# The norms' matrices turned by VectorE's blocks and small transfers instead of TensorE's transposes, in a kernel of six transformer layers and a routed gate

## What is computed

```
xn = layernorm(x)                                   # no weights
s  = xn
for i in range(6):
    n = layernorm(s) * ln1_w[i] + ln1_b[i]
    q, k, v = n @ wq[i], n @ wk[i], n @ wv[i]        # 8 heads of 16
    q = softmax(q, over the 16 of a head);  k = softmax(k, over the tokens)
    s = (q @ (k^T v) per head) @ wo[i] + bo[i] + s
    n = layernorm(s) * ln2_w[i] + ln2_b[i]
    h = n @ w1[i];  h = where(h >= 0, h, 0.01 h)     # 512 wide
    s = h @ w2[i] + s
e = argmax(xn @ router_w + router_b);  w = its softmax weight     # 8 experts
out = x + s * silu((xn @ expert_w[e] + expert_b[e]) * w)
```

## Time and profile before

| what | value |
|---|---|
| median of 3 runs | 653.16 us (651.39 to 653.6) |
| the profiled execution | 654.56 us |
| its span, first to last instruction | 652.7 us |
| mean granted TensorE clock | 0.995 of full |
| busy share of the span: TensorE, VectorE, ScalarE, GpSimd | 97%, 81%, 61%, 46% |
| transfers, mean | 44 GB/s |

### The profile page before, as it was taken

The page is one execution under the profiler, slowest core; times in us unless marked ns, Lnnn a source line. Parts: engine busy times, 40 slices in busy tenths (PEclk is TensorE's granted clock), DMA queues, the critical chain, the costliest instruction groups (busy, mean ns, idle before and its releaser), DMA issues.

```text
span 652.7 us, 13026 instructions
## 1 busy us (share of the span) xinstructions
PE 629.9 (97%) x4598; PEld 568.5 (87%) x4598; DVE 530.0 (81%) x1495; ACT 400.8 (61%) x693; POOL 297.9 (46%) x279
## 2 busy tenths in 40 slices
PE   8788989999999999999999999999999999999996
PEld 8677879889889899898898899899899988889885
DVE  6767989878978879879878878788888788988576
ACT  2746647557657566576566576576675665675563
POOL 4442367678433233333223423322432475786643
PEclk9979999999999999999999999999999999999999
DMA  8920000000102002022002021001020010000003
GB/s 288 313 110 2 1 22 30 25 24 30 54 1 66 1 2 66 2 66 65 1 0 57 7 64 48 17 2 39 27 66 17 1 30 20 18 26 21 21 2 130
DMA packets 29175, 29.03 MB, mean 44 GB/s; under 512 B 3265, under 2 KB 24769, under 8 KB 29122
## 3 DMA queue, kind: packets, MB, share of 16 engines
q1 hardware_dynamic: 26640, 24.12, 11.7%
q0 software_dynamic: 2048, 4.20, 2.2%
q10 hardware_dynamic: 434, 0.02, 0.1%
HBM read 17.85 MB, written 10.49 MB: 43 GB/s over the span
## 4 chain that ended last, share of the span: by engine, by line
PE 86%; DVE 6%; ACT 3%; POOL 2%; issue 1%; DMA 1%; DVEq 0%; ACTq 0%
PE psY L440 25%; PE psT L347 12%; PE psH L352 7%; PE psH L353 6%; PE psH L354 6%; PE psM L537 6%; PE psM L486 6%; PE psT L481 6%; PE psS L512 5%; DVE st L717 1%; PE psS L411 1%; DVE hid L976 1%; PE psS L520 1%; DVE qsum L1079 1%; PE psS L525 1%
## 5 line engine op out<-in xcount | busy, mean ns | idle before, releaser
L440 PEld LDWEIGHTS psY<-w_all,hid 128*128 128x128 f32 x1536 | 195.5, 191 | 18.6 <-issue 8.0
L440 PE MATMUL psY<-w_all,hid 128*128 128x128 f32 (+1 forms) x1536 | 203.4, 276 | 0.2 <-DVE X L948 0.2
L1166 POOL TENSOR_TENSOR rstd<-veps,minus_half 128x8 f32<-128x8 f32 x52 | 85.9, 1652 | 181.0 <-DVE veps L734 180.9
L976 DVE TENSOR_TENSOR hid<-psH,hsl 128x512 f32<-128x512 f32 x192 | 131.1, 684 | 33.7 <-ACT hsl L629 30.9
L629 ACT ACTIVATE hsl<-psH 128x512 f32<-128x512 f32 x192 | 114.3, 596 | 53.0 <-PE psH L354 50.4
L647 ACT ACTIVATE xh<-X,shift,rstd 128x128 f32<-128x128 f32 x280 | 116.9, 487 | 0.4 <-POOL shift L1169 0.3
L1220 POOL TENSOR_TENSOR xn_lo<-xn,xn_hi 128x512 fp32r<-128x512 f32 x46 | 57.8, 1278 | 101.3 <-DVE xn_hi L985 101.3
L352 PE MATMUL psH<-xn_hi,w_hi 128*128 128x512 f32 x184 | 86.1, 468 | 4.1 <-POOL xn_lo L1220 1.6
L717 DVE BATCH_NORM_STATS2 st<-X 128x6 f32<-128x128 f32 x384 | 80.6, 278 | 0.1
L353 PE MATMUL psH<-xn_hi,w_lo 128*128 128x512 f32 x184 | 72.9, 396 | 0.0
L354 PE MATMUL psH<-xn_lo,w_hi 128*128 128x512 f32 x184 | 72.5, 394 | 0.0
(11 more groups left out here) (153 smaller groups left out, 1048.3 us busy)
## 6 DMA issues: line engine op xcount, KB each, us to landing
wb<-expert_rows SPq DMA_DIRECT2D x40, 128.0 KB, 2.1
w_all<-in_w_dram SPq DMA_DIRECT2D x12, 256.0 KB, 4.8
sorted_x<-zeros SPq DMA_DIRECT2D x5, 512.0 KB, 6.4
xs<-sorted_x SPq DMA_DIRECT2D x10, 256.0 KB, 2.9
sorted_y<-ys SPq DMA_DIRECT2D x10, 256.0 KB, 2.4
xraw<-in_x_dram SPq DMA_DIRECT2D x4, 512.0 KB, 5.9
out_dram<-xraw SPq DMA_DIRECT2D x3, 512.0 KB, 2.6
expert_rows<-expert_all SPq DMA_DIRECT2D x1, 1024.0 KB, 8.1
```

The costliest lines, as they stand in the source:

```text
L440: last = nc.tensor.matmul(tile(psY, t), tile(hid[:, i % NC, :], t), of_layer(w2_all, l, c * D, D), start=(c == 0 and t == 0), stop=(c == N ...
L976: nc.vector.tensor_tensor(hid[:, i % NC, :], psH[:, i % 2, :], hsl[:, i % 2, :], ALU.max) \
L1166: nc.gpsimd.tensor_tensor(rstd[:, norm, :], veps[:, norm, :], minus_half[:, :], ALU.pow) \
```

## The change

Both norms' matrices are turned without TensorE. VectorE transposes the 32x32 blocks of the normalised matrix into `blocks1` or `blocks2` (one instruction over 128x1024), and sixteen transfers from SBUF to SBUF (`quadrants`), each of 32 partitions by 1 KB (32 KB), put the block rows where they belong, in `turned1` or `turned2`. ScalarE reads these, in another order of columns, for `xnT` and `xn2`. All the transfers are issued by SP, norm 2's of item s-2 ahead of norm 1's of item s, in `slot(s)`. The first item's norm 1 and the last item's norm 2 are still turned by TensorE.

Slots are written out without a hardware loop, and an item now passes through five: norm 1 in slot s (item s), attention (s-1), norm 2 (s-2), the first part of the FFN (s-3), its last four `output` steps (s-4). There are 27 slots, and the steps' order on each engine is new. ScalarE normalises all eight tiles of norm 1 and makes `xn2_hi`. The attention's product goes to `psT` in place of `psM`. The biases of all layers are computed in slot 1; weights and norm parameters are read where they are loaded, without copies. `zeros` shares its memory with `blocks1`, `expert_all` with `blocks2` and `turned2`, `bvm` with `wb`.

The diff, cut to its core:

```diff
+        Q = 32
+        NQ = P // Q
+        blocks1 = sb("blocks1", [P, T])
+        turned1 = sb("turned1", [P, T])
+        turn2 = sb("turn2", [P, 2, T])
+        blocks2, turned2 = turn2[:, 0, :], turn2[:, 1, :]
...
+        def by_block(a):
+            return a.rearrange("p (t i d) -> p i t d", i=NQ, d=Q)
+
+        def by_tile(a):
+            return a.rearrange("p (j t x) -> p t j x", j=NQ, x=Q)
+
+        def natural(a):
+            return a.rearrange("p (t j x) -> p t j x", j=NQ, x=Q)
+
+        def slots(slot):
+            for s in range(1, ITEMS + 4):
+                slot(s)
 
...
+
+            def quadrants(dst, src, name):
+
+                for j in range(NQ):
+                    for i in range(NQ):
+                        sp.dma_start(dst[i * Q:(i + 1) * Q, j * NT * Q:(j + 1) * NT * Q],
+                                     src[j * Q:(j + 1) * Q, i * NT * Q:(i + 1) * NT * Q]).then_inc(sig(name), 16)
+
+            def feature_major1(n):
+
+                if there(n) and n > 0:
+                    sp.wait_ge(sig("blocks1_ready"), n)
+                    wait(sp, "turned1_ready", 16 * NQ * NQ * (n - 1))
+                    wait(sp, "xnT_ready", n)
+                    quadrants(turned1, blocks1, "turned1_ready")
+
+            def feature_major2(n):
+
+                if there(n) and n < ITEMS - 1:
+                    sp.wait_ge(sig("blocks2_ready"), n + 1)
+                    wait(sp, "turned2_ready", 16 * NQ * NQ * n)
+                    wait(sp, "xn2_ready", n)
+                    quadrants(turned2, blocks2, "turned2_ready")
+
+            def slot(s):
+                groups(s)
+                feature_major2(s - 2)
+                feature_major1(s)
+
...
+                attention(s - 2)
+                if s == 2:
+                    normalised_tiles(2)
+                if s == 3:
+                    ranks()
+                output(s - 4, 4)
+                if group_of(s) is not None:
+                    turn_rows(group_of(s))
+                output(s - 4, 5, 6, 7)
+                hidden(s - 3, 0, 1)
+                if group_of(s) is not None:
+                    apply_expert(group_of(s))
+                keys(s - 1)
+                queries(s - 1)
+                if s == 1:
+                    value_bias()
+                if s == 2:
+                    logits(2)
+                hidden(s - 3, 2, 3)
+                keys_by_token(s - 1)
+                if s == 1:
+                    output_bias(0, range(0, 4))
+                    normalised_tiles(0)
+                if s == 2:
+                    normalised_tiles(3)
+                output(s - 3, 0, 1)
+                last_norm2_by_feature(s - 2)
+                key_sums(s - 1)
+                if s == 1:
+                    output_bias(1, range(4, L))
+                    logits(0)
+                    normalised_tiles(1)
+                if s == 2:
+                    logits(3)
+                output(s - 3, 2)
+                hidden(s - 3, 4)
+                context(s - 1)
+                hidden(s - 3, 5)
+                output(s - 3, 3)
+                mixing(s - 1)
+                queries_by_feature(s - 1)
+                if s == 1:
+                    logits(1)
+                hidden(s - 3, 6, 7)
...
+            def attention_input(n):
+
+                if there(n):
+                    wait(act, "k_done", n)
+                    wait(act, "q_done", n)
+                    if n == 0:
+                        act.wait_ge(sig("t1_done"), 1)
+                        act.wait_ge(sig("param_loaded"), 16 * 2)
+                        nc.scalar.activation(xnT[:, :], psT[:, :], ACT.Identity, bias=param(1, n), scale=param(0, n)) \
+                            .then_inc(sig("xnT_ready"), 1)
+                    else:
+                        act.wait_ge(sig("turned1_ready"), 16 * NQ * NQ * n)
+                        nc.scalar.activation(natural(xnT[:, :]), by_tile(turned1[:, :]), ACT.Identity,
+                                             bias=param(1, n), scale=param(0, n)).then_inc(sig("xnT_ready"), 1)
+
+            def hidden_input(n):
+
+                if not there(n):
+                    return
+                wait(act, "xn2_lo_ready", 2 * n)
+                if n == ITEMS - 1:
+                    act.wait_ge(sig("t2_done"), 1)
+                    nc.scalar.activation(xn2[:, :], psM[:, :], ACT.Identity, bias=param(3, n), scale=param(2, n)) \
                         .then_inc(sig("xn2_ready"), 1)
-
...
+                slope(s - 4, 6, 7)
+                hidden_input(s - 3)
+                if group_of(s) is not None:
+                    rows_by_feature(group_of(s))
+                if s == ITEMS + 2:
+                    silu(3)
+                attention_input(s - 1)
+                if s == 1:
+                    normalise_input(2)
+                if s == 2:
+                    feature_major(2)
+                slope(s - 3, 0, 1)
+                norm2(s - 2, 0)
+                norm2(s - 2, 1)
+                norm2(s - 2, 2)
+                exp_keys(s - 1)
+                slope(s - 3, 2)
+                norm2(s - 2, 3)
+                slope(s - 3, 3)
+                if s == ITEMS + 1:
+                    silu(0)
+                    silu(1)
+                keys_by_token(s - 1)
+                if s == 1:
+                    feature_major(0)
+                if s == 2:
+                    feature_major(3)
+                exp_queries(s - 1)
+                norm1(s, 0)
+                norm1(s, 1)
+                norm1(s, 2)
+                norm1(s, 3)
+                if s == 1:
+                    feature_major(1)
+                    normalise_input(3)
+                slope(s - 3, 4, 5)
...
+            def blocks_of_norm1(n):
+
+                if there(n) and n > 0:
+                    dve.wait_ge(sig("xh1_ready"), 4 * (n + 1))
+                    wait(dve, "turned1_ready", 16 * NQ * NQ * (n - 1))
+                    if n == 1:
+                        dve.wait_ge(sig("rows_zeroed"), 16 * (SLOTS // NT))
+                    nc.vector.transpose(blocks1[:, :], by_block(xh1[:, n % 2, :])).then_inc(sig("blocks1_ready"), 1)
+
+            def blocks_of_norm2(n):
+
+                if there(n) and n < ITEMS - 1:
+                    dve.wait_ge(sig("xh2_ready"), 4 * (n + 1))
+                    wait(dve, "turned2_ready", 16 * NQ * NQ * n)
+                    if n == 0:
+                        dve.wait_ge(sig("sorted_rows_out"), 16)
+                    nc.vector.transpose(blocks2, by_block(xh2[:, :])).then_inc(sig("blocks2_ready"), 1)
+
...
+            def slot(s):
+                add_y(s - 4, 0)
+                leaky(s - 4, 6, 7)
+                if s % NBATCH == 3 and s < ITEMS:
+                    stage_w1(s // NBATCH)
+                add_attention(s - 2)
+                if s == 3:
+                    take_ranks()
+                statistics2(s - 2)
+                if s == 3:
+                    count_tokens()
+                add_y(s - 4, 1)
+                if s == ITEMS + 2:
+                    gated(1)
+                statistics1(s, 0)
+                statistics1(s, 1)
+                leaky(s - 3, 0, 1)
+                if s == 3:
+                    pad_counts()
+                if group_of(s) is not None:
+                    expert_bias(group_of(s))
+                key_maxima(s - 1)
+                variances1(s)
+                query_maxima(s - 1)
+                if s == 1:
+                    value_bias()
+                if s == 3:
+                    first_rows()
+                blocks_of_norm2(s - 2)
+                leaky(s - 3, 2, 3)
+                if s == 1:
+                    output_bias(0, 0, 4)
+                if s == 3:
+                    rows_of_tokens()
+                if s == ITEMS + 1:
+                    gated(0)
+                query_sums(s - 1)
+                scale_key_sums(s - 1)
+                if s == 1:
+                    output_bias(1, 4, L)
+                sum_reciprocals(s - 1)
+                mask_context(s - 1)
+                blocks_of_norm1(s)
+                leaky(s - 3, 4, 5)
+                if s == 4:
+                    experts_of_tiles()
+                    top_weights()
+                if s == ITEMS + 2:
+                    gated(2)
+                finish_mix(s - 1)
+                if s == 2:
+                    route()
+                if s == ITEMS + 3:
```

More of the change, by code:

```diff
@@ L220, in xb, with param @@
         def xb(a, b, lo=0, n=T):
[L222 to L268, removed]
+            return a[:, b, lo:lo + n]
+        def param(k, n):
+            return lnp[:, k, n // NBATCH:n // NBATCH + 1]
+        def by_block(a):
[7 more added lines that the diff above has]
+                slot(s)
         block = ctx.enter_context(nc.Block())
@@ new lines, in value_bias, with output_bias @@
+            def value_bias():
+                pe.wait_ge(sig("attn_loaded"), 16 * 4 * (L - 1))
```

(54 more changed lines are left out.)

693 lines of the change are left out of this document (233 added, 460 removed).

## The result

The changed kernel takes 864.57 us (median of 4, 861.92 to 868.23) against 653.38 us for the kernel before (median of 4, 651.39 to 655.71): a ratio of 1.323, interval 1.316 to 1.331. The forecast was 683 us with a range up to 716. The direction was right; the size was far off, 211 us of loss where 30 were forecast.

What follows compares the result with a forecast made beforehand. TensorE's ordered instructions bound the kernel before; after the change, the circle through SP's queue would. Span 21.75 + 81 + 129 + 239.4 + 154.8 + 56.6 = 682.6, + 1.86 - 1.4 = 683 us; range 640 to 716.

Steps and rivals of the forecast that it cites:

- the circle over `keys`: Path from one `keys` start to the next through DVE, SP's 32 issues, landing and `xnT`: 25.8 us a slot.
- the issue interval: SP's queue issues one transfer every 0.472 us, bounds 0.43 to 0.50; last of 32 starts 14.6 us after the first.
- the clock: Rival, 12%: TensorE's clock falls during waits, keys and queries take 7.0 us: 29.3 a slot, 760 in all, 722 if half.
- the first slots: First three steps of the kernel: 27.5 + 26 + 27.5 = 81 us, against 73.6 before.
- the tail: Time after the last key product to the end of the span: kept at 56.6 us.
- The forecast's own sign of being wrong: In SP's queue, an issue interval other than 0.47 us in the changed profile would show the forecast wrong.
- the landing: Last transfer of norm 1, from issue to arrival: 2.1 us, bounds 1.6 to 2.6.
- The nine slots with groups: Slots 9 to 17, where `groups(s)` frees SP at 8.65 and not 7.85 us after `keys`: 26.6 us each.
- the removed transposes: 46 sets of norm transposes leave TensorE, 0.87 us each: 40 us, 1.74 per slot.
- the rival that it costs double: Rival, 8%: the block transpose on DVE costs double, one in the circle adding 1.2 x 22 = 26 us: 709.
- The transfers are quick enough: Rival, 26%: 32 issues and last landing take 15.6 us or less, so no slower; 643 at 14.9 us.
- The transfers don't matter: Rival, 4%: TensorE stays the bound, all 40 us come back, 23.2 a slot, about 615; needs an interval below 0.37.

Runs made afterwards that it cites:

- Kernel 2: The changed kernel with 40 identity transposes in front of each key product, where TensorE otherwise waits: 830.63 us, ratio 1.268.
- kernel 5: The changed kernel with both norms turned by TensorE again, keeping the new orders and five slots, without block transposes or their transfers: 673.09 us, ratio 1.029.
- Kernel 9: The changed kernel with turnings through DRAM (one store, four loads), plus 10 and 16 identity transposes around the bias products in slot 1: 631.67 us, ratio 0.967.
- kernel 6: The changed kernel with one straight 128x1024 SBUF-to-SBUF transfer per turning in place of sixteen, leaving out the blocks' rearrangement: 633.01 us, ratio 0.968.
- kernel 1: The kernel before the change with seven series of test transfers added at the end of SP's program, where its queue is idle: 656.33 us, single run.
- kernel 7: The changed kernel with each turning as one store to DRAM, a wait and four loads, both norms: 642.04 us, ratio 0.980; second run 635.24, 0.971.

## Why the prediction came out wrong

The mechanism was right: the circle over `keys`, the query maxima, norm 2's blocks, 32 issues, one landing and `xnT` became the path, as the chain shows, and ACT's `xnT` waited 176.4 us in 23 waits, 7.7 each, where 2 to 4 were forecast. The forecast's own sign of being wrong, an interval other than 0.47, is what appeared. The sum failed in the issue interval, the clock, the first slots and the tail.

- **The issue interval: the first step that failed.** The forecast took 0.472 us from the earlier trace rows, loads from DRAM, and bounded it by 0.43 and 0.50, from the same rows. The pieces go from SBUF to SBUF: 0.633, outside the bounds. From the first issue to the last it is 20.6 us (662.71 - 642.15), not 14.6: + 5.9 in this step, in which one issue took 1.59. Over the 20 steady steps it is 20.2 on average, + 5.6 each, 112 us. For the landing I did note that no row had SBUF at both ends and stretched the bound, and there the term held (1.9 us, 2.1 forecast); for the issue I did not. No run has 32 issues a slot at 0.47, so the share of the interval by itself is worked out from the circle and not tried.
- **The clock: a rival that was given 12%.** It had the mechanism and the level right, and a wait of 3 us in mind. With the longer issues the wait is 5 to 7 us, and the clock falls in each step. Kernel 2 measures it in the circle: 10.3 us from `keys` to the first issue, not 7.6 (my term was 7.85, so that one holds at full clock): + 2.5 a step against the forecast, 50 us over 20. The rival's price of 3.5 a step was high; one reason is that the queries' product is back at full speed before its end (2.84 us on the chain, where the earlier trace rows have 1.78). The Trainium skill (TensorE: Matmul & The Clock Gate, HAM oscillation) describes such a fall at every wait for a transfer. This trace agrees, with a median of 1.062 us for a key matmul against 0.592 in kernel 2.
- **The rivals were not independent.** I priced them one at a time, each on top of 683, and the high end of the range by unknown costs without the clock. A longer run of issues makes a longer wait, and the wait costs the clock: 25.8 + 5.9 + 2.5 - 0.2 (the landing) is 34.0, and the step shown took 34.14. With the average of the issues it is 33.7, and the mean of 20 steps is 33.47, against my 26.2: + 146 us.
- **The nine slots with groups** were not longer: 33.3 us a step (298.38 to 597.95), where the other steady ones took 33.6. I had added 0.8 to each (from 8.65; the two terms I gave, 2.6 and 5.96, make 8.56). In the changed kernel the groups' issues are over some 2 us before norm 2's begin (339.57 and 341.72), since those begin 10.3 us after `keys`.
- **The first slots.** I gave 81 us to the first three steps; they took 108.4. Of that, kernel 5 shows that 90.6 come without any of the new transfers. Step 1 took 41.0 us and not 27.5. I let the first blocks wait for the zeroing of `sorted_x`, to about 37 us; they were transposed only at 48.7, behind the work of slot 1 on the chain. The bias products, of which I said "I cost them at nothing", stand on that chain for 7.4 us, from 30.55 to 36.41 and from 41.12 to 42.63, the first of them at a granted clock of 0.50 to 0.53. Kernel 9 got 3 to 4 us back with the clock held up. How the rest of the 17 us divides between the products and the orders was not tried.
- **The tail** took 65.8 us and not 56.6, + 9. Most of that comes without any of the new transfers, too: kernel 5's is 64.1. Where in it was not taken apart.

Together 146 + 27 + 9 = 182 us, against 865.3 - 682.6 = 182.7 of span.

What held: the removed transposes (40 us forecast, 40.1 between kernels 5 and 6); the block transpose (1.22 forecast, 1.234 in the median, so the rival that it costs double is out):

```profile
L1038 DVE STREAM_TRANSPOSE blocks<-xh x23: 1233/1234/1245, 48.7 to 779.9; 128x1024 f32<-128x1024 f32 x23
```

DVE's busy time (530 forecast unchanged, 533.2), `xnT` on ACT (1.2 forecast, 1.24), and SP's two runs with no gap between them. The rule cited from the Trainium skill (DMA: Bandwidth & Descriptors, Rules for kernel authors), one transfer over all partitions rather than several over parts, is borne out as advice: one transfer for each turning gives 633 us, sixteen give 865. Its reason, that the parts share the same engines, is not what these runs show: kernel 1 finds the pieces' issue time the same over 32 and 128 partitions, and what the sixteen cost is time of SP's queue. I let the rule stand beside the sum and not in it, since the cost per transfer was already there; it was the size of that cost which I had from the wrong rows.

The rivals on the faster side are now answered as well. "The transfers are quick enough" asked for 15.6 us or less for the issues and the last landing; they take 22.4 (642.15 to 664.59). "The transfers don't matter" asked for an interval under 0.37 and would have given about 615. (By the circle's own terms 0.39 would do: 31 x 0.39 in place of 14.6 brings 25.8 to 23.3.) Kernel 6, where they don't matter, gives 633: 615 plus the 17 us of the first slots is 632. That this fits so closely is in part luck, since kernel 6 also has a longer tail (59.4 us) and shorter steps (22.93) than the rival assumed.

## What to carry to other kernels

Price a transfer by a row with the same memories at its ends; if there is none, say so of the issue as well as of the landing, and widen the sum by it, multiplied by the number in the circle. When a step depends on one in-order queue, count its instructions first: one store and four loads through DRAM beat sixteen pieces within SBUF by 222 us here, although every byte travels twice. Price both ends of the kernel by themselves when slots and orders are new. And price rivals that cause each other together: a longer wait in front of TensorE also buys a slower TensorE behind it.

## What the hardware showed that was not expected

- In an unbroken run, a transfer issued from SP's queue holds it 0.63 to 0.68 us when both ends are in SBUF and 0.46 us when one is in DRAM, for the numbers of partitions (32, 64, 128 within SBUF; 32 and 128 with DRAM) and bytes (32 and 128 KB) that were tried in kernel 1. A lone one holds it 0.47 us even for 512 KB within SBUF (kernel 6). The loads of `wb`, for which SP first reads the expert's number, take about 0.96 each (3.84 for four), so 0.46 is not the price of every load. Why is open.
- Now and then one issue takes 0.9 to 1.7 us and not 0.6, as at 651.57 in the changed kernel: 17 of the 697 issues that its chain shows. Its cause was not looked for.
- The landing of a 32 KB piece within SBUF, 1.9 us from its issue in the median, is hardly less than the 2.1 us of 128 KB from DRAM; 512 KB from SBUF to DRAM take 6.4 in the zeroing at the start. What is size in that, what memory and what other traffic, these rows don't separate.
- A store to DRAM of 512 KB and four loads from it turn a matrix in 4.6 to 6.3 us of the queue, wait included (kernel 7).
